# The opening of a four-layer transformer block kernel: one set-up semaphore split by part, its work dealt to other engines, and a new timetable for all engines

## The reference, cut to what matters

```python
x = x + attn_a(layernorm(x), W1, b1, Wp, bp)      # 16 heads of 16, causal over 1024 tokens, softmax
x = x + ffn(layernorm(x), w_gate, w_up, w_down)   # hidden 768: silu(gate) * up, then down
x = x + attn_b(layernorm(x), Wq, Wk, Wv, Wo, last_k_init, last_v_init)   # sliding window of 64
x = x + ffn(layernorm(x), w_gate, w_up, w_down)   # the same FFN weights
```

## Time and profile before

| | |
|---|---|
| median of 3 runs | 1241.68 us (1239.53 to 1243.46) |
| profiled execution, its own time | 1242.7 us |
| its span (first to last instruction) | 1240.9 us |
| TensorE busy | 1107.1 us, 89% |
| VectorE busy | 830.3 us, 67% |
| ScalarE busy | 725.8 us, 58% |
| GpSimd busy | 385.0 us, 31% |
| mean granted TensorE clock | 0.977 of full speed |

### The profile page before, as it was taken

How to read it: one execution, slowest core, us unless ns; L and a number is a source line. 1 busy time by engine, 2 the same in 40 slices (tenths; PEclk the granted TensorE clock), 3 DMA queues, 4 the chain that set the end, 5 groups by cost and what they waited for, 6 DMA issues and landing times.

```text
span 1240.9 us, 32317 instructions
## 1 busy us (share of the span) xinstructions
PE 1107.1 (89%) x13339; PEld 670.4 (54%) x13339; DVE 830.3 (67%) x1547; ACT 725.8 (58%) x1038; POOL 385.0 (31%) x385
## 2 busy tenths in 40 slices
PE   4788888998998888999998888899899888899997
PEld 2542336765864224765685332676586422476675
DVE  7788935565687881666688893566568888256652
ACT  2257783566455777456645677456645577745653
POOL 7343223212343324202432322321233332420242
PEclk9889999999999999999999999999999999999999
DMA  7430000122223000113212200012222200011101
GB/s 281 135 134 16 11 11 23 56 74 72 75 71 109 16 11 10 46 58 103 71 36 72 100 12 11 23 56 70 72 79 71 76 16 11 11 46 52 57 19 35
DMA packets 70385, 71.64 MB, mean 58 GB/s; under 512 B 26016, under 2 KB 62304, under 8 KB 69344
## 3 DMA queue, kind: packets, MB, share of 16 engines
q1 hardware_dynamic: 70240, 69.56, 17.0%
HBM read 23.60 MB, written 8.39 MB: 26 GB/s over the span
## 4 chain that ended last, share of the span: by engine, by line
PE 67%; DVE 16%; ACT 7%; issue 4%; POOL 4%; DMA 1%; POOLq 0%; ACTq 0%; DVEq 0%
PE ring L1692 12%; PE ring L1724 7%; PE ring L1659 7%; PE ring L1725 7%; DVE peak L1254 5%; PE ring L1614 5%; ACT probs_causal L1450 4%; PE ring L1738 4%; PE ring L1743 4%; PE ring L1567 3%; DVE xn L1147 2%; PE ring L1568 2%; PE ring L1569 2%; DVE peak_c L1254 2%; POOL h_lo L1122 2%
## 5 line engine op out<-in xcount | busy, mean ns | idle before, releaser
L1254 DVE TENSOR_REDUCE peak<-ring 128x2 f32<-128x1024 f32 (+5 forms) x320 | 324.2, 1032 | 73.1 <-PE ring L1636 30.5
L1450 ACT ACTIVATE probs_causal<-ring 128x1024 f32<-128x1024 f32 (+1 forms) x320 | 286.6, 939 | 128.0 <-PE ring L1659 97.5
L1659 PE MATMUL ring<-q_st,k_st 64*64 64x192 f16 (+5 forms) x2752 | 166.0, 296 | 26.8 <-ACT probs_causal L1450 15.3
L1122 POOL TENSOR_TENSOR h_lo<-h_f,h_hi 128x512 fp32r<-128x512 f32 x96 | 122.9, 1289 | 193.0 <-ACT h_hi L1484 193.0
L1692 PE MATMUL ring<-probs_causal,V 128*32 128x512 f32 (+3 forms) x1536 | 166.5, 511 | 5.5 <-POOL probs_causal L1107 5.0
L1107 POOL TENSOR_SCALAR_AFFINE_SELECT probs_causal<-probs_causal 128x512 f32<-128x512 f32 x128 | 80.9, 635 | 281.9 <-ACT probs_causal L1450 281.7
L1724 PE MATMUL ring<-xf_hi,w_gu_sb 128*128 128x512 f32 x384 | 155.6, 405 | 7.4 <-DVE xf_lo L1154 6.6
L1113 POOL TENSOR_TENSOR onf<-osb,onf 128x512 f32<-128x512 f32 x64 | 81.6, 1276 | 241.1 <-DVE onf L1297 241.1
L1725 PE MATMUL ring<-xf_lo,w_gu_sb 128*128 128x512 f32 x384 | 150.5, 392 | 0.0
L1659 PEld LDWEIGHTS ring<-q_st,k_st 64*64 64x64 f16 x2752 | 65.9, 105 | 154.0 <-ACT probs_causal L1450 57.5
L1322 DVE SCALAR_TENSOR_TENSOR h_f<-ring,gate 128x512 f32<-128x512 f32 x96 | 65.9, 690 | 121.2 <-PE ring L1725 64.1
(11 more groups left out here) (154 smaller groups left out, 1986.4 us busy)
## 6 DMA issues: line engine op xcount, KB each, us to landing
q_st<-q_part SPq DMA_DIRECT2D x96, 128.0 KB
w_qkv<-img_qkv SPq DMA_DIRECT2D x7, 1536.0 KB, 7.7
on_lo<-onf SPq DMA_DIRECT2D x64, 128.0 KB, 2.6
k_st<-k_part SPq DMA_DIRECT2D x48, 144.0 KB, 2.1
k_st<-k_part SPq DMA_DIRECT2D x48, 128.0 KB, 2.1
y<-X SPq DMA_DIRECT2D x8, 512.0 KB, 3.0
wp_sb<-img_wp SPq DMA_DIRECT2D x7, 512.0 KB, 3.4
x_next<-in_x SPq DMA_DIRECT2D x3, 1024.0 KB, 6.2
```

What stands on the lines that cost most here:

```text
L1122: pool.tensor_tensor(h_lo[m][:], h_f[m][:], h_hi[m][:].bitcast(F32), ALU.subtract).then_inc(h_lo_done, 1)
L1254: dve.tensor_reduce(dst, scores, AX.X, ALU.max).then_inc(a_max, 1)
L1450: act.activation(in_banks(block[0:rows, n % slots], unit, w), heads_of(flat_of(a, e), unit, w)[0:rows], ACT.Exp, scale=back[a % 2]).then_i ...
L1659: last = pe.matmul(psum[BLOCK * m:BLOCK * m + BLOCK, r, per * n:per * n + w], keys[rows_of(r), head, first_key + BLOCK * m:first_key + BLO ...
```

## The change

It has three parts.

**Semaphores.** `s_pool` becomes five: `s_ident`, `s_rows`, `s_masks`, `s_xt_edges`, `s_onf`. TensorE waits only for the identity, the first A for masks and edges, the pads' DMAs for their own rows. ScalarE's wait ahead of its first `std` is gone.

**Work.** The identity comes first on GpSimd; the pads' four selects work on one column and one copy spreads it. The ones of `V` and the clearing of `onf` go from GpSimd to ScalarE. The value weights are no longer split with the query and key weights: they need no `alpha`, and form an event `values` of their own (ScalarE's first part, GpSimd's rest). Ten warm-up matmuls behind the first L are gone. GpSimd's late passes over weights and `X` wait for the second half's `xn`.

**Timetable.** All durations in `steps`, the engines' start times (`FREE`), the landings (`LANDED`), and all due times are new, for all layers.

```diff
-            pool.memset(ident[:], 0.0).then_inc(s_pool, 1)
-            pool.memset(mask_f[:], MASKED).then_inc(s_pool, 1)
-            pool.memset(pads[:], 0.0).then_inc(s_pool, 1)
...
+            pool.memset(ident[:], 0.0).then_inc(s_ident, 1)
+            pool.memset(pads[:, 0:1], 0.0).then_inc(s_rows, 1)
...
+            pool.tensor_copy(ident_b[:], ident[:]).then_inc(s_ident, 1)
...
+            pool.tensor_copy(pads[:, 1:KPAD // 2], pads[:, 0:1].to_broadcast([32, KPAD // 2 - 1])).then_inc(s_rows, 1)
...
-            pool.memset(V[:, ONES_BY_DVE:NT + 1], 1.0).then_inc(s_pool, 1)
-            pool.memset(onf[:], 0.0).then_inc(s_pool, 1)
...
+                elif what == "values":
+                    part, hi, lo = of_attention(0)[1], hi_of_attention()[1], lo_of_attention()[1]
+                    pool.wait_ge(s_values, 1)
+                    pool.tensor_tensor(lo, part, hi.bitcast(F32), ALU.subtract).then_inc(s_values, 1)
...
                         pool.wait_ge(s_gu[k], 2)
+                        pool.wait_ge(xn_done[1], 4)
...
                         pool.wait_ge(s_bias, 3)
+                        pool.wait_ge(xn_done[1], 4)
...
-            act.wait_ge(s_pool, SET_BY_POOL - 2)
+            act.activation(ones, table[:, 8:9].to_broadcast([P, ones.shape[1]]), ACT.Identity, bias=1.0).then_inc(s_v_ones, 1)
...
+            act.activation(cleared, table[:, 8:9].to_broadcast([P, cleared.shape[1]]), ACT.Copy).then_inc(s_onf, 1)
...
-                    pe.wait_ge(s_qkv_lo, parts)
+                    pe.wait_ge((s_qkv_lo, s_values)[parts - 1], parts)
...
+                    if a == 0 and sg == 0:
+                        pe.wait_ge(s_masks, 16)
+                        pe.wait_ge(s_xt_edges, 4)
...
-            pe.wait_ge(s_pool, SET_BY_POOL - 2)
+            pe.wait_ge(s_ident, 4)
...
-            run(work[:1])
-            warm_up(10)
-            run(work[1:first])
+            run(work[:first])
...
-LAYER_START = (-10.59, 172.72, 218.56, 506.40, 561.97, 682.58, 727.53, 777.23)
+LAYER_START = (93.43, 161.02, 153.72, 527.89, 502.08, 575.15, 566.57, 604.82)
```

More of the change, by code:

```diff
@@ L576, in needs_of_set_up @@
             return [(("U", "scale", 0), 4)]
+        if what == "values":
+            return [[(("D", "qkv"), 0)], []][step]
         if what in ("att_b", "kpre") and step == 0:
@@ L582, in needs_of_set_up @@
             return [(("F", "gu", PIECES // 4 * (e[2] + 1) - 1), 0)]
+        if what == "gu" and step == 2:
+            return [(("Z", 1), 1)]
         return [] if step else [(("D",) + e[1:], 0)]
@@ L616, in order @@
     meant = timetable(joined)
[L617 removed]
+    free = dict(FREE)
     done, left, follows, known, rank = {}, {}, {}, {}, {}
```

213 lines of the change are left out of this document (113 added, 100 removed), and 207 rows, old and new, of the table TIMES.

## The result

Two sets of four executions on one chip gave 1203.10 us (1196.61 to 1207.85) for the changed kernel and 1240.61 us (1235.26 to 1243.46) for the kernel before: a ratio of 0.9699, with a 95% interval of 0.9642 to 0.9756. The change gains 37 us. The forecast was 1220 us with a range from 1209 to 1234, so the direction was right and the gain 1.8 times as large as predicted.

The account below looks back on a forecast made before the run. TensorE bounds the FFNs; in causal layers TensorE and VectorE wait for one another over PSUM banks; the opening idles. 1242.7 - 9 - 2 - 10.5 = 1221.2 us for the profiled execution, so 1220 us at the median, range 1209 to 1234.

Parts of the forecast that it names:

- The opening, 9 us: Set-up and start of layer 0: with two waits removed, the first A starts at 36.5 instead of 45.80 us.
- Rest of the first causal attention, 2 us: Layer 0 after A's start: query rest and value chunk 1 moved out, exponentials earlier; 2 us gained, from 0 to 5.
- The tail and the places before sliding layers change little: 0, from -2 to 2.: Kernel's end and the passages into sliding-window layers: no gain expected, 0 us, from -2 to 2.
- The joints, 10.5 us: Three FFN-to-causal passages: 22 more A units under the FFN save 3.5 us each, from 0 to 5.
- Table loads at nothing: ScalarE, mostly in FFNs: ten more loads are hidden and cost nothing; without cover, up to 14.9 us.
- Rival "collisions move": Opening: second-half xn and the weights' rest each wait for one GpSimd cast, 4.4 us lost, 1225 us; chance 0.10.

Follow-up runs that it names:

- e1: Kernel before with the changed set-up and order of layer 0 only, the old order in all later layers: 1224.46 us, ratio 0.9891.
- e2: Kernel before with its old set-up and layer 0, the changed order from the end of layer 0's FFN on: 1216.29 us, ratio 0.9831.
- e3: Kernel before with the new opening and layer 0 and the new order in the four sliding-window layers, joints and causal layers old: 1207.93 us, ratio 0.9752.
- e4: Kernel before with the new opening and layer 0 and the new order in the three joints and causal layers, sliding layers old: 1212.22 us, ratio 0.9793.
- e16: Changed kernel with ScalarE's second-half std put back ahead of the first four exponentials in each sliding layer: 1212.91 us, ratio 0.9779.
- e13: Kernel before with the new opening and layer 0 and the new order only in the three joints: 1231.64 us, ratio 0.9911.
- e17: Kernel before with the new opening and layer 0 and the new order only in the second half of causal layers 2, 4, 6: 1225.59 us, ratio 0.9884.
- e10: Changed kernel with twelve more ScalarE table loads, two ahead of each of six gates in the FFNs of layers 1, 3, 5: 1217.17 us, ratio 0.9830.
- J: Segment used in hybrids: the three joints, each a sliding layer's FFN plus the next causal attention's first half; new with the new opening only, 1231.64 us (e13).
- e11: Changed kernel with one useless 64x64 quarter-array matmul ahead of each of the 192 gate and up units: 1247.46 us, ratio 1.0069.
- e8: Changed kernel with two useless GpSimd passes beside the second half's four xn: 1202.35 us in one execution.
- C: Segment used in hybrids: second half of causal attention and most of that layer's FFN, three times; new with the new opening only, 1225.59 us (e17).
- e9: Changed kernel without its 185 planned filler matmuls, the five of the warm-up kept: 1218.09 us, ratio 0.9832.
- e14: Changed kernel with each filler group two matmuls shorter, 128 of 185 fillers left: 1202.39 us, ratio 0.9681.
- e15: Changed kernel with each filler group at half its length, 90 of 185 fillers left: 1215.64 us, ratio 0.9795.
- e12: Changed kernel with one useless 128x64 full-tiling matmul ahead of each of the 192 gate and up units: 1218.45 us, ratio 0.9830.

## Why the prediction was wrong, step by step

- **The opening, 9 us.** Right in mechanism and size. First A at 36.07 us, and one late wait put back moves it by 4.4 us and the whole by 5. With the next term the forecast was 11 us; e1 measured 14, 13 at equal clock, and the step from e2 to the changed kernel 12 at equal clock.
- **Rest of the first causal attention, 2 us.** The trace had 7.3 (the end of the causal attention 17.0 us earlier, A 9.7). The kernel times, 12 to 14 us less the 9.7 of A, say 2 to 4. The size was a little low, within its bounds of 0 to 5.
- **"The tail and the places before sliding layers change little: 0, from -2 to 2."** This is the step that failed. It measured 12 to 17 us: 16.5 from e1 to e3, 14.8 at equal clock, and 12.7 at equal clock from e4 to the changed kernel. The prediction gave no reason for the zero: I had read the FFN as full by its busy share, and read no window of the sliding layer itself. What the runs show in its place is the start of each sliding layer, from the last down projection to the first V: 16.21 us before and 13.97 after in layer 3, some 11 us over four layers. Two things differ there: TensorE has the scores directly behind the down projection, and ScalarE has four exponentials ahead of a `std` that waits for `mv`. e16 puts back the second alone, and 8.7 us are lost; 4 to 6 us more are left to other edits of the same segment that I did not separate. In the trace of before the fillers counted as busy and the 6.06 us of `std` were signs, but neither by itself gave the price.
- **The joints, 10.5 us.** The size was about right (12.2 measured from e1 to e4, 8.0 at equal clock, 6 to 8 over both ways), the mechanism only half. Moving the A units under the FFN loses 3 us without the new order of the second half (e13), and that order alone gives nothing (e17). The sum was also too kind: 16.5 us of maxima don't fit in the 14.8 us that VectorE had free there.
- **Table loads at nothing.** Too low: 1.0 us each on average where two stand ahead of a gate (e10). In the net sum of the joints it doesn't show. J brings six loads and 18 changes of tiling, 6 and 2 us as an estimate by e10's and e11's prices; that these turn J alone into a loss is argued, and no run shows it.
- **Rival "collisions move".** The lock is real (e8), but the changed kernel's opening hardly meets it: its four `xn` take 1.38 us and the weights' rest 1.21.
- **The sum.** At equal clock, opening 13, sliding 15, causal 6 (from e3 to the changed kernel: 1207.7 to 1201.8) make 34, and 3.5 us come of the clock.

Open are the split inside the sliding layers beyond e16, what C alone gives back, and whether the second half of layer 0 has 0 or 4 us.

## What to carry to other kernels

Busy share does not show that a stretch is full: count fillers as idle, and look for the in-order engine whose head waits for something late while ready work stands behind it. One `std` ahead of four exponentials cost 2.2 us at each of four places, as much as a joint with the half layer behind it (2 to 2.7 us at each of three). Ask also whether that work is ready: in the kernel before it wasn't, and two engines' orders had to change together. When two changes to an order act on one shared idle time, price them together: either alone may give nothing. And when the granted clock differs from execution to execution, keep it beside each time: here, with it, the scatter within a kernel was 1.6 us.

## What the runs showed of the hardware

- Most of what a lower granted clock takes from TensorE shows in the time: 0.001 of mean clock is, as an estimate, 2.4 us of the 1200 at the lower of the two levels (1.2 GHz), which is 1.2 us of lost full speed, and it goes with 0.89 us.
- With 185 matmuls without use, 0.38 us each, the mean clock is 0.984; without them it is 0.956. With 128 of them it is 0.983, with 90 it is 0.969 (means over the executions of the changed kernel, e9, e14 and e15).
- A change of tiling between full and quarter array costs about 0.1 us (e11 less e12, 29.0 us over 280 changes).
- A VectorE `tensor_scalar` beside back-to-back GpSimd passes waits for one pass each time: 4.50 instead of 1.38 us for four (e8).
